# Seven half-height border blocks in the expert stage, longer filler, and paired chunks in an adaLN, attention and MoE kernel

## The reference

```
h = layernorm(x) * (1 + ca) + sa
x = x + ga * attention(h)            # one head of 128, softmax over 2048 keys
h = layernorm(x) * (1 + cb) + sb
x = x + gb * ffn(h)
ffn: shared = down(silu(gate(h)) * up(h))                      # I = 512
     scores, idx = top_k(sigmoid(h @ router.T + bias), 2)      # 8 experts
     out = shared + sum over the 2 chosen of normalised score * expert_e(h)
```

## Time and profile before

| | |
|---|---|
| runs | 1611.42, 1612.41, 1612.57 us, median 1612.41 |
| profiled execution | 1612.66 us; span 1611.1 us; mean granted clock 0.996 |
| PE | 1582.4 us busy, 98% of the span, 12578 matmuls |
| DVE | 1188.3 us, 74% |
| ACT | 997.8 us, 62% |
| POOL | 547.9 us, 34% |
| DMA | 168.75 MB, mean 105 GB/s |

### The profile page before, as it was taken

One profiled execution on the slowest core, in us unless ns is written; L12 is line 12 of the kernel. 1 busy time (PEld: TensorE's weight loads), 2 busy tenths in 40 slices (PEclk: granted clock), 3 DMA queues, 4 the chain that ended last, 5 costly groups with the idle time before them and its releaser, 6 DMA issues.

```text
span 1611.1 us, 37339 instructions
## 1 busy us (share of the span) xinstructions
PE 1582.4 (98%) x12578; PEld 1524.2 (95%) x12579; DVE 1188.3 (74%) x2444; ACT 997.8 (62%) x1735; POOL 547.9 (34%) x607
## 2 busy tenths in 40 slices
PE   8999999999999999999999999999999999999998
PEld 7799999999999998999999999999999999999997
DVE  6677787778777787888776666666666666666587
ACT  5566666666665656666655666666666666666653
POOL 2546645332300001477761222222222222222231
PEclk9999999999999999999999999999999999999999
DMA  4233343421101325432243132133123231111697
GB/s 126 85 121 125 128 139 122 139 79 46 40 27 34 138 112 166 152 120 97 100 151 96 61 104 63 58 110 112 56 92 105 82 111 58 60 56 50 182 299 187
DMA packets 72298, 168.75 MB, mean 105 GB/s; under 512 B 13188, under 2 KB 18692, under 8 KB 71560
## 3 DMA queue, kind: packets, MB, share of 16 engines
q1 hardware_dynamic: 47560, 102.35, 18.8%
q0 software_dynamic: 23248, 62.97, 13.2%
q10 hardware_dynamic: 1392, 2.10, 0.4%
HBM read 95.99 MB, written 71.39 MB: 104 GB/s over the span
## 4 chain that ended last, share of the span: by engine, by line
PE 51%; POOL 4%; DVE 2%; issue 2%; DMA 2%; ACT 0%; POOLq 0%; DVEq 0%; ACTq 0%; SPq 0%
PE f_bank L981 31%; PE f_bank L32 5%; PE f_bank L34 5%; PE f_bank L33 5%; POOL x_rows L1453 4%; PE f_bank L963 2%; PE f_bank L954 1%; DMA y_rows<-more_rows,goes_to 1%; DMA w_all<-y_rows 1%; DVE Z L1974 1%; DVE w_all L1967 1%; PE f_bank L1630 0%; PE f_bank L1632 0%; DVE f_prod L1036 0%; PE f_bank L1647 0%
## 5 line engine op out<-in xcount | busy, mean ns | idle before, releaser
L981 PE MATMUL f_bank<-xT_hi,w_cur_hi 128*128 128x256 f32 x1136 | 321.6, 283 | 0.9 <-ACT f_silu_g L1016 0.9
L981 PE MATMUL f_bank<-xT_hi,w_cur_lo 128*128 128x256 f32 x1136 | 321.5, 283 | 0.0
L981 PE MATMUL f_bank<-xT_lo,w_cur_hi 128*128 128x256 f32 x1136 | 321.5, 283 | 0.0
L1471 POOL DMA_INDIRECT y_rows<-more_rows,goes_to x142 | 138.9, 978 | 439.3 <-ACT more_rows L1574 252.5
L1036 DVE TENSOR_TENSOR f_prod<-f_silu_g,f_bank 128x512 f32<-128x512 f32 x206 | 141.6, 687 | 111.9 <-PE f_bank L981 109.3
L1959 DVE TENSOR_TENSOR w_cur_lo<-w_all,w_cur_hi 128x1024 fp32r<-128x1024 f32 x142 | 173.5, 1222 | 63.4 <-ACT w_cur_hi L1541 63.3
L981 PEld LDWEIGHTS f_bank<-xT_hi,w_cur_hi 128*128 128x128 f32 x1136 | 217.8, 192 | 1.0 <-issue 1.0
L981 PEld LDWEIGHTS f_bank<-xT_hi,w_cur_lo 128*128 128x128 f32 x1136 | 218.1, 192 | 0.0
L981 PEld LDWEIGHTS f_bank<-xT_lo,w_cur_hi 128*128 128x128 f32 x1136 | 217.9, 192 | 0.0
L981 PE MATMUL f_bank<-xT_hi,w_shared 128*128 128x256 f32 x1024 | 202.7, 286 | 0.5 <-PEq L58 0.5
L441 ACT ACTIVATE prob<-s_pair,negmax 128x1024 f32<-128x1024 f32 x128 | 142.1, 1114 | 89.5 <-DVE negmax L794 89.5
(11 more groups left out here) (304 smaller groups left out, 4389.5 us busy)
## 6 DMA issues: line engine op xcount, KB each, us to landing
more_rows<-x_rows POOLq DMA_DIRECT2D x71, 260.0 KB, 3.0
XS<-in_x SPq DMA_DIRECT2D x32, 256.0 KB, 3.1
XR<-in_x SPq DMA_DIRECT2D x32, 256.0 KB, 2.9
x<-XR SPq DMA_DIRECT2D x32, 256.0 KB, 2.2
Z<-x SPq DMA_DIRECT2D x4, 2048.0 KB, 12.2
w_all<-y_rows SPq DMA_DIRECT2D x32, 256.0 KB, 6.9
w_all<-y_rows POOLq DMA_DIRECT2D x32, 256.0 KB, 7.2
out<-Z SPq DMA_DIRECT2D x31, 256.0 KB, 5.9
```

The costliest lines, as they stand in the source:

```text
L981: mm = pe.matmul(out[:, 2 * P * i:2 * P * i + 2 * P], w, x, start=(c == 0 and n == 0), stop=(c == HC - 1 and n == 2))
L1471: pool.indirect_dma_start(d.y_rows, bass.IndirectOffsetOnAxis(ap=goes_to[:, par, t:t + 1], axis=0), y[:, t, :], None).then_inc(y_sent[t], 16)
```

## The change

Three parts.

**Border blocks.** All experts' sorted rows are still covered by 71 blocks, but only 64 are full. Seven, at j = 4, 14, ..., 64 (`TURN` = 10, `BORDER_AT` = 4), have 128 rows: the half block next to the end of each of the first seven experts. In such a block gate and up have 128 columns, `turn_two` two transposes, `down_two` one tile, and ACT writes one output; POOL loads 128 rows and issues, for the second tile's scatter, a DMA of one row. A border's weights are not in w_all: ACT's queue loads them in the step r = 1 of each ten (`load_border`), raw gate and up and the down parts, to where the shared weights lie; `load_shared` brings these back at step 66. `pairs` now has 10 steps ahead of the loop, a body of 10 run five times, and 11 behind. SP's loads go by turns (`turn_expert`, experts that have a full block). The padding rows come by eight DMAs rather than one. The down parts of the experts have a DRAM tensor of their own. The plan has 48 operations, not 27, and is spread otherwise.

```diff
     def pe_turn_two(pe, m, rows, ready, value, tiles):
...
-            for t in range(2):
+            for t in range(tiles):
...
-        flat = lambda t, c: t[:, k // 2 % 2, c, :, :].rearrange("p t n -> p (t n)")
+        flat = lambda t, c: t[:, k // 2 % 2, c, 0:tiles, :].rearrange("p t n -> p (t n)")
...
-                        mm = pe.matmul(out[:, 2 * P * i:2 * P * i + 2 * P], w, x, start=(c == 0 and n == 0),
+                        mm = pe.matmul(out[:, 2 * P * i:2 * P * i + tiles * P], w, x, start=(c == 0 and n == 0),
...
         def pairs(eng, step):
-            for j in range(4):
-                step(j, j % 2)
-            with eng.Fori(2, NP // 2 - 1) as i:
-                step(2 * i, 0)
-                step(2 * i + 1, 1)
-            for j in range(NP // 2 * 2 - 2, NP):
-                step(j, j % 2)
+            for j in range(TURN):
+                step(j, j, 0)
+            with eng.Fori(1, BORDERS - 1) as i:
+                for r in range(TURN):
+                    step(TURN * i + r, r, i)
+            for j in range(TURN * (BORDERS - 1), NP):
+                step(j, j % TURN, j // TURN)
...
+        def short(r):
+            return r % TURN == BORDER_AT
+        def tiles_of(r):
+            return 1 if short(r) else 2
...
+                    if t == tiles:
+                        pool.dma_start(d.y_rows[2 * T:2 * T + 1, :], d.pad[0:1, 0:H]).then_inc(y_sent[t], 16)
+                        continue
...
+            def load_border(i):
+                after = ALL if isinstance(i, int) and i == 0 else 2 * TURN * i + (ALL + 2 * (BORDER_AT + 1 - TURN))
+                act.wait_ge(f.y_mm, after)
+                e = act.value_load(d.border_expert[0:1, at(i)], min_val=0, max_val=E - 1)
+                for part in range(2):
+                    act.dma_start(d.border_raw[:, W * part:W * part + W],
+                                  d.raw[part][ds(e, 1)].rearrange("o p n -> p (o n)")).then_inc(border_ready, 16)
+                act.dma_start(d.border_down[:].bitcast(F32),
+                              d.down_parts[ds(e, 1)].rearrange("o p a n -> p (o a n)")).then_inc(border_ready, 16)
+            def load_shared():
+                act.wait_ge(f.y_mm, ALL + 2 * (TURN * (BORDERS - 1) + BORDER_AT + 1))
...
                 if n == STEPS + 2:
                     plan_counts()
+                    plan_ends()
                 if n == STEPS + 3:
-                    plan_ends()
+                    plan_starts()
+                    plan_borders()
                 if n == STEPS + 4:
-                    plan_starts()
                     plan_behind()
                 if n == STEPS + 5:
+                    plan_turns()
+                if n == STEPS + 6:
                     plan_experts()
-                if n == STEPS + 6:
                     plan_moves()
+                if n == STEPS + 7:
                     plan_rows()
```

```diff
             pe.wait_ge(d.s_const, d.n_const)
-            keep_busy(pe, d, y_bank, 7)
+            keep_busy(pe, d, y_bank, 9)
```

```diff
-            n = 0 if i < 4 else 1 if i % 2 and 9 < i < LATE - 3 else 2
...
+    FIRST_PAIR = LATE - CHUNKS // 2
...
+            def gate_chunks(k):
...
+                for c in (k, k + 1):
+                    dve.wait_ge(y_sum[c % SLOTS], 16 * (c // SLOTS + 1))
+                two = slots[:, k % SLOTS:k % SLOTS + 2].rearrange("p r t h -> p (r t) h")
+                gate = rows[:, C * k // TB, 0:H].unsqueeze(1).to_broadcast([P, 2 * C, H])
+                dve.tensor_tensor(two, two, gate, ALU.mult).then_inc(gated_done, 1)
...
-                for k in chunks_of[i]:
-                    gate_chunk(k)
-                    output_chunk(k, ALL + max(0, i - 2))
+                if i >= FIRST_PAIR:
+                    gate_chunks(2 * (i - FIRST_PAIR))
+                    output_chunks(2 * (i - FIRST_PAIR), ALL + i - 2)
```

More of the change, by code:

```diff
@@ L955, in pe_turn_rows, with pe_turn_two @@
         mm.then_inc(f.xT_mm, 1)
-    def pe_turn_two(pe, m, rows, ready, value):
+    def pe_turn_two(pe, m, rows, ready, value, tiles):
         pe.wait_ge(ready, value)
@@ L988, in pe_pair_gate_up, with pe_pair_down @@
                             small()
-    def pe_pair_down(pe, t, homes, weights, parts=(0, 1)):
+    def pe_pair_down(pe, t, homes, weights, parts=(0, 1), counts=1):
         hi, lo = weights[2]
@@ L1186, in ffn_phase @@
     SLOTS = 8
-    chunks_of, k = [], 0
-    for i in range(LATE):
-        n = 0 if i < 4 else 1 if i % 2 and 9 < i < LATE - 3 else 2
-        chunks_of.append(range(k, k + n))
-        k += n
-    assert k == CHUNKS
+    FIRST_PAIR = LATE - CHUNKS // 2
+    assert FIRST_PAIR >= 4 and SLOTS % 2 == 0
     PIECE = I
@@ L1574, in output, with step @@
                 act.activation(y[:, t, :], f.y_bank[t][:, 0:H], ACT.Copy, scale=score[:, par, t:t + 1]
-                               ).then_inc(y_copied, 1)
+                               ).then_inc(y_copied, 3 - tiles)
             who = []
-            def step(j, par):
+            def step(j, r, i):
+                par = r % 2
                 if par == 0:
-                    who[:] = experts(act, j)
+                    who[:] = experts(act, r, i)
+                if r == 1 and not (isinstance(i, int) and i == BORDERS):
+                    load_border(i)
+                if isinstance(j, int) and j == TURN * (BORDERS - 1) + BORDER_AT + 2:
+                    load_shared()
                 (m, k), (m1, k1) = (place_of(j, par, n) for n in range(2))
@@ L1676, in turn, with turn_two, down_two @@
                                    vt_done if after_single else None, HC * s)
-            def turn_two(j, par):
+            def turn_two(j, par, tiles):
                 f.pe_turn_two(pe, 2 * j + ALL, lambda c, t: h[:, par, t, P * c:P * c + P], h_in[par],
-                              16 * half(j, par) + 16)
-            def down_two(j, par, e):
+                              16 * half(j, par) + 16, tiles)
+            def down_two(j, par, e, tiles=2):
                 m, k = place_of(j, par, 0)
                 columns = lambda o: lambda c: d.w_all[:, ds(e & 1, 1), o + H * c:o + H * c + H]
+                down = (columns(2 * W), columns(3 * W)) if tiles == 2 else columns_of(d.border_down, W, 0, H)
                 pe.wait_ge(f.aT_lo_done, m + 2)
-                for t in range(2):
+                for t in range(tiles):
                     if inside(j - 1, NP):
@@ L1692, in down_two @@
                         pe.wait_ge(f.y_out, ALL - 1 + t)
-                    f.pe_pair_down(pe, t, (home(k), home(k + 1)), (None, None, (columns(2 * W), columns(3 * W))))
+                    f.pe_pair_down(pe, t, (home(k), home(k + 1)), (None, None, down), counts=3 - tiles)
             def bank_free(m):
@@ L1908, in plan_behind @@
             def plan_behind():
                 op(dve.tensor_tensor(behind, c.numbers[:].unsqueeze(2).to_broadcast([P, B, E]),
-                                     ends[:].unsqueeze(1).to_broadcast([P, B, E]), ALU.is_ge))
+                                     ends[:].unsqueeze(1).to_broadcast([P, B, E]), ALU.is_gt))
+                op(dve.tensor_reduce(behind_end[:], behind[:, 0:NP, :].rearrange("p m e -> p e m"), AX_X, ALU.add))
+                op(dve.tensor_tensor(of_borders(behind), side[:].unsqueeze(2).to_broadcast([P, BORDERS, E]),
+                                     c.experts[:].unsqueeze(1).to_broadcast([P, BORDERS, E]), ALU.is_gt))
@@ L2154, in layer @@
     d.matrices += [one_row(down_w[e]) for e in range(E)]
[L2155 removed]
+    d.raw = [a.rearrange("e p a b -> e p (a b)") for a in (gate_w, up_w)]
     with ExitStack() as ctx:
```

272 lines of the change are left out of this document (174 added, 98 removed).

## The result

The changed kernel takes 1632.94 us (median of 1631.69, 1632.94 and 1634.21), against 1612.41 before: a ratio of 1.014, 95% interval 1.0126 to 1.0154. It is 20.5 us slower where I forecast 1611.4 and no change, and it lies outside my range. Its profiled span is 1631.4 us, 20.3 more than before.

| stretch | before, us | after, us | difference | my terms |
|---|---|---|---|---|
| to the first shared tile | 623.0 | 620.3 | -2.7 | +0.7 |
| shared tiles, routing, entry, to the experts' first transposes | 220.3 | 224.9 | +4.6 | +4.5 |
| expert stage, to the first matmul of the last | 652.0 | 666.3 | +14.3 | -9.3, +1.5 (clock), 0 (loop) |
| last stage | 115.8 | 119.8 | +4.0 | +1.3 |

The account below looks back on a forecast made before the run. PE was taken to bound the expert stage, but not its entry or the last stage, which runs through DVE. Terms -9.3 + 4.5 + 1.5 + 1.3 + 0.7 = -1.3 gave 1611.4 us, no tellable change; range 1603.5 to 1620.0.

Parts of the forecast that it names:

- +1.5 (clock): Entry of the expert stage: PE's longer idle wait drops the granted clock once, 3 us at half speed, +1.5 us.
- The loop: Expert stage: a ten-step body with four jumps back instead of 31 costs 0.
- the jumps miss: Expert loop: instruction fetches at each jump, about 2 us each, +8 us for four, 1619.4 us; chance 0.11.
- The border blocks: Expert stage: seven 128-row blocks save 1.33 us each (0.38 gate and up, 0.22 transposes, 0.73 down), -9.3 us.
- rival that time goes with columns: Border gate and up: 128 columns take half of 0.120 us, another -17.5 us, 1593.9 us at best; chance 0.03.
- The border loads: Expert stage: 2 MB a border, at a DMA share of 0.25, covered by three steps between issue and use: 0.
- Plan and entry: Entry of the expert stage: longer plan, with plan_rows behind the split, moves the first transposes from 843.26 to 847.7, +4.5 us.
- Chunks: Last stage: chunks two at a time, seven odd tiles with a pair at a 10.23 us period, together +1.3 us.
- the -0.7 for the last two tiles: End of the last stage: the last two tiles, not hidden by PE, are 0.35 us shorter each, -0.7 us.
- The rival of the DMA: Last stage: at 285 GB/s a pair's 3.15 MB take 11.05 us, not 10.23; +5.7 us, 1617.1 us; chance 0.13.
- Filler: Prologue: two more fillers push the matmuls behind them by 0.9 - 0.16, +0.7 us.

Follow-up runs that it names:

- border_once: Changed kernel, steps written out, border weights loaded whole for the first border only, a sixteenth of the columns for the others: 1722.87 us, ratio 1.0048 to the kernel before.
- early_plan: Changed kernel, steps written out, plan's table ready ahead of the split of the first block's weights: 1719.79 us, ratio 1.0020 to the kernel before.
- best_singles: Changed kernel, steps written out, early table, old chunk schedule, border weights in three portions: 1599.34 us against 1611.59, ratio 0.9915 to the kernel before.
- before_unrolled: Kernel before with its 71 expert steps written out instead of looped: 1612.93 us, ratio 1.0002 to the kernel before.

## Why the prediction was wrong, point by point

**The loop** is the step that failed. I wrote "Nothing at the jumps of now shows on a PE that is always busy: 0, and a rival below", and put the jumps in the sum at 0. The rows of a two-step body said nothing of a ten-step one, and the four jumps measured +17.2. My rival "the jumps miss" had the mechanism and the sign with a chance of 0.11, and its size was half: 2 us a jump where 4.3 were measured. I had priced it as three fetches of 0.76 us on one engine that PE follows, from q14 alone; the other instruction queue of the profile's page, q8 with 64 packets, I left out. PE itself stops, for 3.10 us at the first jump, and I left out that the clock can fall behind such a stop (1.76 us more there), though I had counted just that at the entry. ACT, one of the three engines that I named, doesn't stop. Without the jumps 20.5 - 17.2 = +3.3 would be left, for the -1.3 of my sum.

**The border blocks.** Measured -8.1 in the loop and 1.5 a block, -10.5, where the steps are written out; forecast -9.3. The way was as worked out: of the down product's 1.42 I kept 0.73 behind two waits for w_cur_lo, and what is left is 0.8 written out and 0.35 in the loop, where both waits show. The 0.112 a matmul held. The chain of the changed kernel has a full half and a short one in a piece:

```profile
888.44 5.51 PE f_bank L983 x48
```

Less 2.88 for the full half, 2.63 is left, 0.110 a matmul. The rival that time goes with columns is out. The 81 ns of the Trainium skill, "TensorE: Matmul & The Clock Gate", Back-to-back issue gap, are not reached here: the rows have 110 and 112.

**The border loads** I had at 0. The issue was hidden but for the first time, when ACT's third DMA issue took 2.30 us and the step 10.74, and contention with POOL's scatter added up to 3.7 in three more steps (border_once puts it at 2 to 5 us where the steps are written out). I had set the contention at 0 by an average DMA share of 0.25, which says nothing about a burst.

**Plan and entry.** +4.6 for +4.5, and the clock +2.1 for +1.5: right in mechanism and size, and early_plan and best_singles are without both. (Thirteen operations at 0.2 are 2.6 and not 2.8, a slip of 0.2 us.) That the clock would fall was less sure than it looks: it fell behind all seven entry waits of 4.9 to 5.1 us in these traces, but also behind one of 2.43 in before_unrolled, and not behind the 2.28 of before.

**Chunks.** +4.0 for +1.3. DVE's period is as worked out (10.2: down products at 1551.78, 1561.96 and 1572.18), and up to the last tile the loss is +1.9 for my +2.0. The step that failed is the -0.7 for the last two tiles: they came out at +2.1, because the last pair waits 2.10 us for its chunk's load and PE's last down products stand behind it. The rival of the DMA named the resource, but put it in the seven periods and at 5.7 us. How much of this waiting is due to a pair needing both chunks, and how much to the later start, wasn't tried apart.

**Filler.** I had +0.7; what showed was -2.7, in the main of a two-valued start that both fillers have. What sets which start comes is open.

## What to carry to other kernels

Before a loop body is made longer, ask what each engine executes in it: here a body of six steps jumped free, and one of ten stopped PE and DVE for about 3 us a time and mostly took the clock with it, which ate more than the whole saving. Look for it as "issue" ahead of the first instruction of the body and as packets of the instruction queues inside the loop, and try the loop's form alone in the old kernel. And a saving on the bounding engine counts only net of the bursts, plans and starts that are moved to make it: the same idea with the steps written out, the table early, the loads in portions and the old chunk schedule gave 0.85% where it had cost 1.4%.

## What the runs showed of the hardware that I had not expected

A jump back did not get dearer by degrees: DVE lost nothing visible at 2 and 6 steps and about 3 us at 10. ACT, with hardly fewer instructions (about 310 in ten steps against DVE's 350), was not stopped. The five traces with a ten-step body have 20 jumps back, and PE stopped at each, for 2.3 to 3.6 us. In the 3 us behind the stop the granted clock was 0.50 to 0.76 at 16 of them and 1.00 at the other four, whose stops were 2.31, 2.60, 2.88 and 3.29 us: the length of the stop doesn't tell which. And on two chips the kernel before took 116 and 104 us more, with a granted clock of about 0.8 between 650 and 960 us in the traces there, in its shared tiles.
